# Flamingo layer on one core: the rounded queries of the first attention made by ScalarE, and the way into the second attention and its halves laid out as single units

## The reference

```
x += tanh(g_xattn[0]) * cross_attention(LN(x), ctx)   # q,k,v,o projections with biases, 16 heads, 154 keys, stablemax
x += tanh(g_ffn[0])   * (top8_of_64_experts(LN(x)) + shared_swiglu(LN(x)) * sigmoid(gate))
x += tanh(g_xattn[1]) * softmax_attention(LN(x), ctx, ctx)   # no projections, no scale
x += tanh(g_ffn[1])   * (butterfly_down(gelu(butterfly_up(LN(x) @ W_exp + b) + b)) @ W_con + b)

stablemax(s): t = where(s >= 0, s + 1, 1 / (1 - s));  t / sum(t)
```

## Time and profile before

| | us |
|---|---|
| median of 3 executions | 1137.24 (1136.22 to 1138.7) |
| the profiled execution's own time | 1139.42 |
| its span in the trace | 1137.6 |
| PE busy | 989.6 (87%) |
| DVE busy | 777.7 (68%) |
| ACT busy | 622.1 (55%) |
| POOL busy | 402.9 (35%) |

### The profile page before, as it was taken

One profiled execution on the slowest core, in us unless ns is written; L12 is line 12 of the kernel. 1 busy time (PEld: TensorE's weight loads), 2 busy tenths in 40 slices (PEclk: granted clock), 3 DMA queues, 4 the chain that ended last, 5 costly groups with the idle time before them and its releaser, 6 DMA issues.

```text
span 1137.6 us, 16837 instructions
## 1 busy us (share of the span) xinstructions
PE 989.6 (87%) x5379; PEld 702.5 (62%) x5379; DVE 777.7 (68%) x1951; ACT 622.1 (55%) x1204; POOL 402.9 (35%) x417
## 2 busy tenths in 40 slices
PE   4899999999769699998999758788898989989988
PEld 2355555555447488776887636466667666757657
DVE  4688989987787566657675666866775676664443
ACT  1887888879465245546554213654554555454532
POOL 6000111102020257677776222152525252504234
PEclk9899999999979899999999958899999999999999
DMA  6737466453114378888876533413231412110000
GB/s 139 205 73 214 141 175 171 109 151 112 56 52 152 107 175 192 195 231 209 211 178 133 131 85 100 100 35 113 58 94 28 113 51 86 29 49 1 21 19 19
DMA packets 101559, 128.38 MB, mean 113 GB/s; under 512 B 31136, under 2 KB 73504, under 8 KB 101216
## 3 DMA queue, kind: packets, MB, share of 16 engines
q1 hardware_dynamic: 87088, 106.32, 32.8%
q0 software_dynamic: 12288, 18.88, 9.3%
q10 hardware_dynamic: 2096, 2.10, 0.8%
HBM read 66.15 MB, written 30.70 MB: 85 GB/s over the span
## 4 chain that ended last, share of the span: by engine, by line
PE 54%; DVE 22%; ACT 9%; issue 5%; POOL 4%; DMA 3%; SPq 1%; ACTq 1%; DVEq 0%; POOLq 0%
PE psum L960 6%; PE psum L1144 6%; PE psum L1129 5%; PE psum L1049 4%; PE psum L976 4%; PE psum L867 3%; PE psum L838 3%; DVE peaks L1825 3%; DVE stats L1421 2%; PE psum L913 2%; PE psum L784 2%; PE psum L827 2%; PE psum L1076 2%; PE psum L862 2%; DVE weights L1557 2%
## 5 line engine op out<-in xcount | busy, mean ns | idle before, releaser
L1924 POOL TENSOR_SCALAR vareps<-moments 128x4 f32<-128x4 f32 x32 | 12.2, 382 | 350.0 <-DVE moments L1431 350.0
L838 PE MATMUL psum<-q_stack,k_stack 97*128 97x512 f32 (+1 forms) x256 | 118.3, 488 | 20.2 <-DVE weights L1557 7.2
L1355 ACT ACTIVATE weights<-psum 128x512 f32<-128x512 f32 x160 | 92.9, 595 | 65.6 <-PE psum L838 57.5
L1947 POOL DMA_INDIRECT expert_sums<-made,sum_rows x64 | 104.1, 1626 | 63.6 <-DVE made L1789 44.4
L1076 PE MATMUL psum<-k_stack,q_stack 96*128 96x308 f32 x256 | 86.3, 399 | 36.5 <-DVE peaks L1825 24.6
L1557 DVE SCALAR_TENSOR_TENSOR weights<-weights,psum 128x512 f32<-128x512 f32 x160 | 102.7, 681 | 17.8 <-ACT weights L1205 17.5
L1825 DVE TENSOR_REDUCE peaks<-psum 128x2 f32<-128x308 f32 x256 | 105.8, 470 | 7.7 <-PE psum L1076 7.5
L1979 POOL TENSOR_TENSOR hidden<-hidden_whole,hidden 128x512 fp32r<-128x512 f32 x64 | 82.9, 1300 | 60.7 <-DVE hidden L1873 60.7
L960 PE MATMUL psum<-feat_parts,w_shared_up 128*128 128x512 f32 x384 | 98.4, 406 | 4.2 <-DVE shared_silu L1663 2.6
L1076 PEld LDWEIGHTS psum<-k_stack,q_stack 96*128 96x128 f32 x256 | 50.8, 203 | 81.7 <-DVE peaks L1825 40.1
L1144 PE MATMUL psum<-w_con_high,hidden 128*128 128x256 f32 x512 | 100.7, 295 | 0.5 <-POOL hidden L1979 0.5
(11 more groups left out here) (210 smaller groups left out, 2219.9 us busy)
## 6 DMA issues: line engine op xcount, KB each, us to landing
expert_w<-in_expert_w SPq DMA_DIRECT2D x64, 384.0 KB
q_stack<-q_stage SPq DMA_DIRECT2D x96, 128.0 KB, 2.4
q_stack<-q_stage SPq DMA_DIRECT2D x174, 64.0 KB, 2.0
expert_sums<-zeros SPq DMA_DIRECT2D x6, 1408.0 KB, 8.6
fetched<-expert_sums SPq DMA_DIRECT2D x14, 512.0 KB, 4.5
k_raw<-in_k SPq DMA_DIRECT2D x16, 300.0 KB
x<-in_x SPq DMA_DIRECT2D x8, 512.0 KB, 4.8
rows_scratch<-rows SPq DMA_DIRECT2D x8, 512.0 KB, 3.5
```

The source lines that it names most:

```text
L838: T.matmul(to, keys_of(h, head), q[0:row, head // 2, :], start=True, stop=True).then_inc(scored, 1)
L1355: A.activation(weights1[n % 6][:, :], score_bank[n % 2], ACT.Exp).then_inc(exped, 1)
L1947: G.indirect_dma_start(sum_dram[e % SUMS], bass.IndirectOffsetOnAxis(ap=sum_rows[:, e:e + 1], axis=0), made[e % 4][:, :], None, bounds_che ...
```

## The change

ScalarE's program gets the function `q_high` and DVE's loses it. On ACT it is an activation Identity with the bias vector. The slots in the four tables, the string `TAIL` and `WEIGHTS_AT` (how many sets ahead of the end the shared weights' split stands) change. The written-out way in becomes the list `PROLOGUE`, in which each unit stands alone, ("late",) being a step of the shared feed-forward; `burst` goes, and `beside` mixes what a chunk has in the order two of the FFN's units, one peak. In the diff the row of `PROLOGUE` is left out; its order is shown below.

```diff
-WEIGHTS_AT = (6,)
-TAIL = 'lhhlplhllhlhplphllhphlllphlplsplllhhphplpphlhhpllplplphphphhlhllshphsphpsphshpphshpphhpshsphphpspsppts'
+WEIGHTS_AT = (10,)
+TAIL = 'llhlplhllhplhphhhlphlllllphplplllhsphhplhpllphphplllhhppphhplphlsshphshplsphhppphsphphhhspsphphppptsss'
...
-Q_AT = (-34, -25, -24, -21, -21, -20, -19, -19, -17, -17, -17, -16, -16)
...
+Q_AT = (-33, -25, -23, -21, -21, -20, -19, -19, -17, -17, -17, -16, -16)
...
-PEAKS_AT = (-2, -1, 0, 1, 3, 4, 5, 6, 9, 9, 9, 9, 13, 13, 13, 13)
...
+PEAKS_AT = (-5, -4, 0, 1, 4, 4, 6, 7, 9, 9, 9, 9, 13, 13, 13, 13)
...
-BURST_AT = (9, 13)
-
-KEPT_BACK, KEPT_BACK_AT = (HALVES - 2, 1), (2, 2, 5, 5)
+Q1_AT = (0, 6, 10, 11, 12, 12, 13, 18, 19)
+F_AT = (3, 5, 8, 10)
+UP_AT = (9, 9, 9, 9, 13, 13, 13, 13)
+OUT_AT = (9, 10, 11, 12, 13, 15, 15, 15)
+
+KEPT_BACK = (HALVES - 2, 1)
+KEPT_BACK_AT = (4, 4, 7, 8)
...
-def burst(h, b, peak):
-
-    up = [("up", h, BURST * b + k) for k in range(BURST)]
-    peak = peak + [None] * (4 - len(peak))
-    first = None if (h, b) == KEPT_BACK else ("out", h, b, 0)
-    units = [up[0], up[1], peak[0], up[2], peak[1], up[3], peak[2], first, peak[3]]
-    return [u for u in units if u]
...
-        if c == 0:
+        if c == Q1_AT[0]:
...
+        if c == Q1_AT[2]:
             units += norm_units("q1", h + 2)[:2]
...
-        if c == 13:
-            units += [("send_q1", h + 2, 0), ("send_q1", h + 2, 1)]
-        if c in (16, 19):
-            units.append(("send_q1", h + 2, 2 + c // 19))
+        units += [("send_q1", h + 2, two) for two in range(4) if c == Q1_AT[5 + two]]
...
-        if c == 2:
+        if c == F_AT[0]:
...
-        for b, at in enumerate(BURST_AT):
+        work = []
+        for k, at in enumerate(UP_AT):
             if c == at:
-                return units + burst(h - 1, b, peak)
-            if at < c < at + BURST and (h - 1, b) != KEPT_BACK:
-                units.append(("out", h - 1, b, c - at))
+                work.append(("up", h - 1, k))
+        for k, at in enumerate(OUT_AT):
+            if c == at and (h - 1, k // BURST) != KEPT_BACK:
+                work.append(("out", h - 1, k // BURST, k % BURST))
+        mixed = []
+        while work or peak:
+            mixed += work[:2] + peak[:1]
+            work, peak = work[2:], peak[1:]
+        units += mixed
         if h == HALVES:
             units += [("out", *KEPT_BACK, k) for k in range(BURST) if c == KEPT_BACK_AT[k]]
     return units + peak
...
-    late.step()
-    plan += [("add_experts", 0, i) for i in range(SUMS)] + [("fetch", 1)] + norm_units("q1", 0)[:2]
-    late.step()
-    plan += [("key_split1", 0, 0), ("load_k1", 0, 2)] + norm_units("q1", 0)[2:]
-    plan += [("key_split1", 0, 1), ("load_k1", 0, 3)]
-    late.step()
...
-    beside_peaks = {4: norm_units("q1", 1)[:2], 7: norm_units("q1", 1)[2:],
-                    9: [("turn_q1", 1), ("send_q1", 1, 0), ("send_q1_a", 1, 1)]}
-    for n in range(HT * PAIRS // 2):
-        plan.append(("peak", 0, n % HT, n // HT))
-        plan += beside_peaks.pop(n, [])
-        if n in LATE_AT:
+    for unit in PROLOGUE:
+        if unit == ("late",):
             late.step()
-    plan.append(("peaks", 0))
...
-    plan += peak_units(1, -1)
-    plan.append(("scores1", 0))
+        else:
+            plan.append(unit)
     for n in range(20 * (HALVES + 1)):
         h, c = divmod(n, 20)
...
@@ -1193,6 +1177,17 @@
                 for c in range(CD):
                     evacuate(misc, ("turn_q", h), q_feats[:, c, :], c).then_inc(misc.frees(("turn_q", h), c), 1)
 
+            def q_high(h, mo):
+                key = ("project_q", h, mo)
+                if mo == 0:
+                    if h:
+                        wait_all(A, q_in[(h - 1) % 2], (h - 1) // 2 + 1)
+                    else:
+                        A.wait_ge(wq_in, 32)
+                A.wait_ge(*misc.filled(key))
+                A.activation(q_stage[:, 0, mo, :], misc.ap(key), ACT.Identity,
+                             bias=bq[:, mo:mo + 1]).then_inc(queries_rounded, 1)
+
...
@@ -1537,14 +1532,6 @@
                                         by(bv[r, :])[:, j::4, :], ALU.add)
                 m.then_inc(misc.frees(key), 1)
 
-            def q_high(h, mo):
-                key = ("project_q", h, mo)
-                if h and mo == 0:
-                    wait_all(V, q_in[(h - 1) % 2], (h - 1) // 2 + 1)
-                V.wait_ge(*misc.filled(key))
-                V.tensor_scalar(q_stage[:, 0, mo, :], misc.ap(key), bq[:, mo:mo + 1], None,
-                                ALU.add).then_inc(queries_rounded, 1)
-
```

More of the change, by code:

```diff
@@ L191, in route_steps @@
                                      [[("load_expert", e) for e in range(3)] + [("load_fusing",)]] if h == HALVES - 1 else [])
-Q_AT = (-34, -25, -24, -21, -21, -20, -19, -19, -17, -17, -17, -16, -16)
-K_AT = (-19, -18, -15, -7, -6, -5)
-A_AT = (24, 25, 25, 26, 25, 26, 25, 26, 26, 27, 27, 30, 29, 30)
-R_AT = (33, 33, 33, 35, 35, 36, 38, 39, 40, 40, 40, 42, 43, 44, 50, 54)
+Q_AT = (-33, -25, -23, -21, -21, -20, -19, -19, -17, -17, -17, -16, -16)
+K_AT = (-19, -17, -17, -6, -6, -6)
+A_AT = (24, 25, 25, 26, 25, 26, 25, 26, 26, 28, 28, 30, 29, 32)
+R_AT = (33, 33, 33, 35, 35, 36, 37, 38, 39, 39, 40, 42, 43, 44, 49, 56)
 def plan_first():
@@ L403, in beside @@
                 units.append(("load_v1", b))
-        if c in KEYS_AT:
-            n = KEYS_AT.index(c)
+        for n in [n for n, at in enumerate(KEYS_AT) if c == at]:
             units.append(("key_split1", b, n))
@@ L427, in beside @@
     return units + peak
+PROLOGUE = [('add_experts', 0, 0), ('late',), ('add_experts', 0, 1), ('rstd', 'q1', 0), ('fetch', 1), ('stats', 'q1', 0), ('key_split1', 0, 0), ('load_k1', 0, 2), ('late',), ('norm', 'q1', 0), ('key_split1', 0, 1), ('late',), ('load_k1', 0, 3), ('send_q1', 0, 1), ('turn_q1', 0), ('send_q1', 0, 0), ('load_v1', 0), ('key_split1', 0, 2), ('add_experts', 1, 0), ('late',), ('key_split1', 0, 3), ('add_experts', 1, 1), ('lay_rest', 0), ('send_q1_a', 0, 2), ('peak', 0, 0, 0), ('peak', 0, 1, 0), ('peak', 0, 2, 0), ('peak', 0, 3, 0), ('peak', 0, 0, 1), ('send_q1_a', 0, 3), ('peak', 0, 1, 1), ('stats', 'q1', 1), ('peak', 0, 2, 1), ('send_q1', 1, 0), ('peak', 0, 3, 1), ('late',), ('rstd', 'q1', 1), ('peak', 0, 0, 2), ('peak', 0, 1, 2), ('norm', 'q1', 1), ('peak', 0, 2, 2), ('turn_q1', 1), ('send_q1_a', 1, 1), ('peak', 0, 3, 2), ('send_q1', 1, 3), ('peak', 0, 0, 3), ('peak', 0, 1, 3), ('peak', 0, 2, 3), ('peak', 0, 3, 3), ('peaks', 0), ('peak', 1, 0, 0), ('late',), ('send_q1', 1, 2), ('peak', 1, 1, 0), ('peak', 1, 2, 0), ('scores1', 0), ('peak', 1, 3, 0)]
 def plan_last():
@@ L1398, in scalar_program @@
             A.preload_act_table_set("abs_reciprocal_sqrt_and_small")
-            units = {"key_round": key_round, "send_keys": send_keys, "lay_wk": lay_wk, "q_feats": q_feats_, "square": square,
+            units = {"key_round": key_round, "send_keys": send_keys, "lay_wk": lay_wk, "q_feats": q_feats_, "q_high": q_high, "square": square,
                      "root": root, "keep": keep, "att_feats": att_feats, "row_feats": row_feats_, "gate_exp": gate_exp,
@@ L1888, in vector_program @@
             set_masks()
-            units = {"bn": bn, "highest": highest_, "ranks": ranks, "q_high": q_high, "q_low": q_low, "stats": stats_, "norm": norm, "key_mask": key_mask, "bias_parts": set_bias_parts, "key_rest": key_rest,
+            units = {"bn": bn, "highest": highest_, "ranks": ranks, "q_low": q_low, "stats": stats_, "norm": norm, "key_mask": key_mask, "bias_parts": set_bias_parts, "key_rest": key_rest,
                      "set_values": set_values, "weight": weight,
```

25 lines of the change are left out of this document (9 added, 16 removed).

## The result

The changed kernel takes 1126.15 us (median of 4, 1123.32 to 1127.59) against 1137.51 before: ratio 0.9891, interval 0.9869 to 0.9913, so 12.4 us faster (9.9 to 14.9). The forecast was 1122.3 with a range to 1132.5, so the time lies in it; several of the terms behind it do not hold.

A forecast was written before the change was run, and what follows sets the result against it. PE was taken as the bound, with DVE close behind in the first attention. Terms summed to -14.9 us from the profiled 1139.4, giving 1124.5; less 2.2 to match the median, 1122.3 us, range 1112.5 to 1132.5.

The forecast's parts named there:

- Start: First keys' sends on ACT, now behind the second rounded query: 0 us, at most +3 if the keys land last.
- Rounded queries and attention 1: First attention, 65 to 293 us: rounding moved to ACT shortens chain links and part of DVE's root waits goes; -2.5 us.
- fourth rival: First attention: rounded query waits in ACT's queue with roots ready behind it; +15.3 us there, 1140.1 in all; chance 0.09.
- Way out: 293 to 335 us: less waiting for half 7's divide (-1.0) and less norm stall beside POOL's pair (-2.0); -3.0 us.
- lists' term: 335 to 376 us: two gate-and-up steps moved behind the last places fill PE's wait for the lists' trip; -2.3 us.
- stall's -2.0: Way out of first attention: half 7's norm escapes POOL's pair, 3.9 us of stall, half taken back by hot masks.
- second rival: Way out: stall moved, not removed; POOL's pair delays hot masks by its whole 4.72 us; 1125.1 us; chance 0.15.
- Way in: 640 to 700 us: wait behind ACT's sends mostly goes (-5.5), first peak 1.9 later, shared down step -0.8; -4.4 us.
- norm's lead of 2.0: Into the second attention: norm 2.0 us earlier, its half's first sum preceding a shared step, offsetting the later send's 3.9.
- Halves: Second attention, 700 to 1090 us: reordered bursts remove three of PE's 21 waits for peaks; -2.0 us.
- End: A kept-back output step fills part of a 1.79 us wait at 1108.13; -0.7 us.
- third rival: Halves of second attention: two thirds of peak waits and some hidden-layer waits go, -12.0 us; 1112.3 in all; chance 0.15.

The follow-up runs named there:

- e11: Kernel before with only the last two shared steps ahead of the lists moved behind them in TAIL; ratio 0.9972, -3.2 us.
- e10: Kernel before with only the first shared step (split of half 0) moved four letters later in TAIL; ratio 1.0007, +0.8 us.
- e7: Changed kernel with the sends of half 0's first two pairs of heads in the other order; 1122.66 us, ratio 0.986 against before.
- e4: Kernel before with only the new order of the second attention's halves; ratio 1.0007, +0.8 us.
- e8: Changed kernel with the rounded queries back on DVE at the same slots; 1118.89 us, ratio 0.9825 against before.
- e12: Changed kernel with rounded queries back on DVE and the sends of half 0's first two pairs swapped; 1115.58 us, ratio 0.9799 against before.

## Why the prediction was right or wrong

**Start.** 0 holds as far as a trace tells: the first weighting starts at 32.4 (32.9 before, 30.7 to 33.6 in all 14).

**Rounded queries and attention 1.** -2.5, measured +1.3 in the stage. The step that failed is "on the chain projection, high part, low part, projection, each link shrinks by 0.15". It compared durations only, and with the 687 ns measured even those differ by 0.06 and not 0.15, 0.8 us in all. The link now goes to another engine's queue and back: ACT comes to it late, and the prediction priced ACT's wait (the fourth rival) but not DVE's own new wait, for the low part, with the weighting queued behind: 14.8 us in eleven waits. The fourth rival had the place and half the mechanism; its price of 15.3 was over three times the 4.5 measured, and DVE's wait for roots grew by 1.6, not 12; the new slots gave 2.9 back. The prediction's own sign for this step was that attention 1 must not end later than before: the last weighting starts at 291.2 in place of 290.4.

**Way out.** -3.0 for its first part and -2.3 for the lists, measured -8.3 together (75.7 for 84.0). The lists' term had the mechanism and a size off: by e11 it is 3.4. The last places came the 4.0 earlier that it took, but PE's three steps behind them took 8.1 us where it counted 9.2, and PE waited for nothing where it foresaw 1 to 3 us. The stall's -2.0 failed: e10 shows 0. It was taken from the norm to masks that are needed as soon, whole. The second rival was right in that, and so was the rule of the Trainium skill that it named ("SBUF — State Buffer", section "🔬 SBUF: two separate sides"): 4.3 us lost in e10, 3.0 in the changed kernel. What moved the first part by 4.4 to 4.9 was something else in TAIL, which stays open.

**Experts.** Not in the sum at all. The trace has -2.4, inside the 276.7 to 281.4 of the 14 traces of this plan; what moves it is not shown.

**Way in.** -4.4, measured -2.6 from the last gate-and-up matmul to the first scores (the -5.0 from the tokens takes in the experts). Both mechanisms were there: the wait of 5.85 is gone, and the first peak is late by 4.0 (8.4 for 4.4 us after that matmul) where 1.9 was counted. e7 gives 3.8 of the 4.0 to the order of the sends. The norm's lead of 2.0 did not come off that gap: the turning of the queries starts 0.8 us ahead of the last twelve gate-and-up matmuls in both kernels, so step and norm moved together.

**Halves.** -2.0, measured about 0: e4 gives +0.8 by its ratio with an interval from -1.7 to +3.3, and the stage 398.9 to 402.6 with the new order, 398.7 to 402.2 with the old. PE's waits in the changed kernel, and one of the kernel before that stands beside the earlier trace rows:

```profile
PE psum L1060 <- DVE peaks L1812: 13.5, 15, 2.3
PE psum L1060 <- ACT hidden_whole L1379: 6.5, 11, 0.6
...
PE psum L1113 <- DVE peaks L1812: 3.0, 7, 0.7
PE psum L1113 <- ACT hidden_whole L1379: 2.5, 12, 0.6
PE psum L768 <- DVE peaks L1812: 1.8, 6, 0.7
...
PE psum L768 <- DVE normed L1469: 0.7, 2, 0.3
```

```profile
PE psum L784 <- DVE normed L1474: 3.2, 4, 1.3
```

The ups wait 3.9 less for the hidden layer and 3.0 more for peaks: 18.3 for peaks in place of 15.4, where the prediction said 13. Much of the wait changed its name, but not all: 2.5 of the wait for the next queries' norm went too. Between the first and the last scores PE idles 37.1 to 40.4 us in the six traces with the new order and 42.1 to 43.2 in the eight with the old, so waits did go, as the prediction counted. The step that failed is that a wait gone is time won: PE's busy time, for the same matmuls, is 360.4 to 362.1 us with the new order and 355.9 to 359.2 with the old, and the stage is no shorter. The ends of matmuls are modelled in these traces, and why they fill the freed time is not shown.

**End.** -0.7. Both traces of the changed kernel have -1.0, but four others with the same order (e4, e7, e8, e12) have 43.2 to 43.7 for the 43.5 before. Not shown.

So the total was near (-14.9 against -12.4) because misses cancelled: 3.8 too much hoped for in attention 1, 1.8 in the way in and 2.0 in the halves, against 3.0 more in the way out and 2.4 behind it. That is luck: both surpluses come in the main from causes that the prediction did not name and the runs do not settle.

One bound was drawn askew as well: the range is said to take in the third rival's centre, 1112.3, but starts at 1112.5.
